# A mixture-of-experts kernel's first transfers and warm-up moved ahead of its engine block, and its last wait moved behind it

## What is computed

```python
def _L0_cond_ref(h, gating_probs, shared_gate_prob, Wg, Wu, Wd, Sg, Su, Sd):   # E, F = 8, 512
    g = jnp.einsum('bsd,edf->ebsf', h, Wg)
    u = jnp.einsum('bsd,edf->ebsf', h, Wu)
    expert_outs = jnp.einsum('ebsf,efd->ebsd', jax.nn.silu(g) * u, Wd)
    expert_output = jnp.einsum('be,ebsd->bsd', gating_probs, expert_outs)
    shared = jnp.einsum('bsf,fd->bsd', jax.nn.silu(h @ Sg) * (h @ Su), Sd)
    sg = shared_gate_prob[:, :, None]
    return (1.0 - sg) * expert_output + sg * shared
x = x + _L0_cond_ref(x, fside_Bx8_0, condB_sharedgateprob[:, None], ...)       # x: (16, 128, 128) f32
x = x + jnp.einsum('bij,bjk->bik', T[itok_B_1_98 - 1], x)
```

## Time and profile before

| | |
|---|---|
| median of 3 runs | 307.45 us (307.35 to 308.07) |
| the profiled execution's own time | 307.27 us |
| its span, first to last instruction of the program | 305.4 us |
| time of that execution outside the span (307.27 - 305.4) | 1.87 us |
| PE busy | 302.0 us, 99% of the span |
| DVE, ACT, POOL busy | 70%, 54%, 34% |

### The profile page before, as it was taken

How to read it: one execution, slowest core, us unless ns; L and a number is a source line. 1 busy time by engine, 2 the same in 40 slices (tenths; PEclk the granted TensorE clock), 3 DMA queues, 4 the chain that set the end, 5 groups by cost and what they waited for, 6 DMA issues and landing times.

```text
span 305.4 us, 4487 instructions
## 1 busy us (share of the span) xinstructions
PE 302.0 (99%) x1348; PEld 250.4 (82%) x1348; DVE 214.1 (70%) x347; ACT 163.8 (54%) x306; POOL 104.8 (34%) x119
## 2 busy tenths in 40 slices
PE   8999999999999999999999999999999999999996
PEld 7888888888888888888888888888888888888885
DVE  4777667766776676667766776677676667787873
ACT  5755555555555555555555555555555555554563
POOL 3687114431244115511551134411451155710010
PEclk9999999999999999999999999999999999999999
DMA  6700200030002000110003000003000000013243
GB/s 192 264 2 1 103 3 0 0 104 0 0 0 103 0 0 0 31 72 0 0 0 112 26 26 26 26 25 106 0 0 2 0 0 0 2 34 69 38 103 103
DMA packets 14186, 12.00 MB, mean 39 GB/s; under 512 B 7008, under 2 KB 12384, under 8 KB 14176
## 3 DMA queue, kind: packets, MB, share of 16 engines
q1 hardware_dynamic: 14032, 11.81, 12.6%
q10 hardware_dynamic: 144, 0.07, 0.1%
HBM read 10.04 MB, written 1.84 MB: 39 GB/s over the span
## 4 chain that ended last, share of the span: by engine, by line
PE 99%; ACT 0%; issue 0%
PE o_bank L499 11%; PE o_bank L496 11%; PE o_bank L497 11%; PE u_bank L468 11%; PE u_bank L470 11%; PE u_bank L469 11%; PE g_bank L468 11%; PE g_bank L470 11%; PE g_bank L469 11%; PE o_bank L535 1%; PE o_bank L514 0%; PE g_bank L514 0%; PE u_bank L514 0%; PE g_bank L542 0%; PE u_bank L509 0%; PE u_bank L542 0%
## 5 line engine op out<-in xcount | busy, mean ns | idle before, releaser
L374 DVE TENSOR_TENSOR u_bank<-u_bank,silu_g 128x512 f32<-128x512 f32 x144 | 100.7, 699 | 82.0 <-PE u_bank L470 81.1
L303 ACT ACTIVATE silu_g<-g_bank 128x512 f32<-128x512 f32 x144 | 86.3, 599 | 132.8 <-PE g_bank L470 132.7
L266 POOL TENSOR_TENSOR acc<-acc,scaled 128x512 f32<-128x512 f32 x32 | 41.4, 1295 | 180.5 <-DVE scaled L388 180.5
L380 DVE TENSOR_TENSOR h_lo<-u_bank,h_hi 128x512 fp32r<-128x512 f32 x144 | 98.1, 681 | 0.1
L309 ACT ACTIVATE h_hi<-u_bank 128x512 fp32r<-128x512 f32 x144 | 85.6, 594 | 0.4 <-DVE u_bank L374 0.4
L499 PE MATMUL o_bank<-h_lo,w_hi 128*128 128x512 f32 x144 | 56.1, 390 | 0.0
L496 PE MATMUL o_bank<-h_hi,w_hi 128*128 128x512 f32 x144 | 56.1, 390 | 0.0
L497 PE MATMUL o_bank<-h_hi,w_lo 128*128 128x512 f32 x144 | 56.0, 389 | 0.0
L469 PE MATMUL u_bank<-x_lo,w_hi 128*128 128x512 f32 x143 | 55.6, 389 | 0.0
L468 PE MATMUL u_bank<-x_hi,w_hi 128*128 128x512 f32 x143 | 55.6, 389 | 0.0
L470 PE MATMUL u_bank<-x_hi,w_lo 128*128 128x512 f32 x143 | 55.6, 389 | 0.0
(11 more groups left out here) (64 smaller groups left out, 145.8 us busy)
## 6 DMA issues: line engine op xcount, KB each, us to landing
w_raw<-in_W_all SPq DMA_DIRECT2D x8, 768.0 KB, 4.4
T_plus<-in_TT SPq DMA_DIRECT2D x16, 64.0 KB, 1.7
turned_y<-yB SPq DMA_DIRECT2D x3, 256.0 KB, 2.3
y<-turned_y SPq DMA_DIRECT2D x12, 64.0 KB, 2.3
acc<-in_xT SPq DMA_DIRECT2D x2, 256.0 KB, 3.6
acc<-in_xT SPq DMA_DIRECT2D x1, 512.0 KB, 5.9
out_y<-res SPq DMA_DIRECT2D x2, 256.0 KB, 2.3
out_y<-res SPq DMA_DIRECT2D x3, 128.0 KB, 1.9
```

The lines of the kernel that those rows point to most:

```text
L266: nc.gpsimd.tensor_tensor(acc[:, t, :], acc[:, t, :], scaled[:, t % 2, :], ALU.add).then_inc(acc_done, 1)
L303: nc.scalar.activation(silu_g[:, k % 2, :], g_bank[k % 2][:, :], ACT.Silu).then_inc(g_read, 1)
L374: nc.vector.tensor_tensor(u_bank[k % HR][:, :], u_bank[k % HR][:, :], silu_g[:, k % 2, :], ALU.mult).then_inc(h_done, 1)
L380: nc.vector.tensor_tensor(h_lo[:, k % HR, :], u_bank[k % HR][:, :], h_hi[:, k % HR, :].bitcast(F32), ALU.subtract).then_inc(split_done, 1)
```

## The change

Three things are moved. The transfers of x tile 0 and of chunk 0's gate and up weights, which SP issued first in its part of the block, are issued in front of the block. The eight warm-up matmuls are too. The wait for the seven stores goes from the end of SP's part to behind the block.

```diff
-        block = ctx.enter_context(nc.Block())
+        nc.sync.dma_start(acc[:, 0, :], xT[0, :, :]).then_inc(x_in[0], 16)
+        nc.sync.dma_start(w_raw[:, 0, 0, 0:2, :], W_gu0[:, :, :]).then_inc(wc0_in[0], 16)
+
+        nought = nc.const_aps.tensor(0.0, (P, P), F32)
+        for _ in range(8):
+            nc.tensor.matmul(o_bank[1][:, 0:P], nought, nought, start=True, stop=True)
+
+        with nc.Block() as block:
...
-            load_x(0, 1, x_in[0])
-            sp.dma_start(w_raw[:, 0, 0, 0:2, :], W_gu0[:, :, :]).then_inc(wc0_in[0], 16)
...
-            sp.wait_ge(stored, 16 * 7)
...
-            def warm_up(n):
-
-                for _ in range(n):
-                    nc.tensor.matmul(o_bank[1][:, 0:P], nought, nought, start=True, stop=True)
-
-            nought = nc.const_aps.tensor(0.0, (P, P), F32)
-            warm_up(8)
...
+        nc.sync.wait_ge(stored, 16 * 7)
```

More of the change, by code:

```diff
@@ L207, in _ @@
[L207 to L294, removed]
-            add_group(E * NT - 1, NT - 1)
@@ L297, in _ @@
-        @block.scalar
-        def _(act):
-            def silu(n, k):
-                act.wait_ge(g_done, n + 1)
-                nc.scalar.activation(silu_g[:, k % 2, :], g_bank[k % 2][:, :], ACT.Silu).then_inc(g_read, 1)
-            def round_h(n, k):
-                act.wait_ge(h_done, n + 1)
-                nc.scalar.activation(h_hi[:, k % HR, :], u_bank[k % HR][:, :], ACT.Copy).then_inc(h_rounded, 1)
-            def copy_y(i):
-                b, nb = parts[i]
-                act.wait_ge(y_turned, i - SINGLE + 1)
-                nc.scalar.activation(y[:, b:b + nb, :], part_bank(i)[:, 0:nb * D].rearrange("p (b d) -> p b d", b=nb),
-                                     ACT.Copy).then_inc(y_done, 1)
-            def round_x(t):
-                act.wait_ge(x_in[min(t, 2)], 16)
-                nc.scalar.activation(x_hi[:, t, :], acc[:, t, :], ACT.Copy).then_inc(x_rounded, 1)
-            def round_w0(c, m):
-                nc.scalar.activation(w_hi[:, 0, c, m, :], w_raw[:, 0, c, m, :], ACT.Copy).then_inc(w0_rounded, 1)
-            act.wait_ge(zero_done, 1)
-            nc.scalar.activation(silu_0[:, :], zero[:, 0:1], ACT.Silu)
-            act.wait_ge(wc0_in[0], 16)
-            for m in range(2):
-                round_w0(0, m)
-            act.wait_ge(wc0_in[1], 16)
-            round_w0(1, slice(0, 2))
-            silu(0, 0)
-            act.wait_ge(wd0_in, 16)
-            round_w0(slice(0, 2), 2)
-            silu(1, 1)
-            round_h(0, 0)
-            round_w0(slice(2, NC), 2)
-            round_x(1)
-            for n in range(2, PEEL_ACT):
-                silu(n, n)
-                round_h(n - 1, n - 1)
-                if n >= PEEL_ACT - 2:
-                    round_x(NT - PEEL_ACT + n)
-            with act.Fori(0, N - U, U) as n0:
-                for k in range(PEEL_ACT, U + PEEL_ACT):
-                    silu(n0 + k, k)
-                    round_h(n0 + k - 1, k - 1)
-            for n in range(N - U + PEEL_ACT, N + 1):
-                if n < N:
-                    silu(n, n)
-                round_h(n - 1, n - 1)
-            def copy_late(i):
-                b, nb = parts[i]
-                act.wait_ge(r_done, i + 1)
-                nc.scalar.activation(res[:, b:b + nb, :], part_bank(i)[:, 0:nb * D].rearrange("p (b d) -> p b d", b=nb),
-                                     ACT.Copy).then_inc(late_done, 1)
-            copy_late(1)
-            copy_late(HALF)
-            for i in range(SINGLE, len(parts)):
-                copy_y(i)
-            copy_late(SINGLE + 1)
-            copy_late(SINGLE + 3)
-            act.wait_ge(late_done, 4)
-            act.dma_start(out[:, B - 1:B, :], res[:, B - 1:B, :]).then_inc(stored, 16)
@@ L464, in _ @@
-        @block.tensor
-        def _(pe):
-            def product(bank, w, x_h, x_l, start, stop):
-                nc.tensor.matmul(bank, w_hi[:, w[0], w[1], w[2], :], x_h, start=start, stop=False)
-                nc.tensor.matmul(bank, w_hi[:, w[0], w[1], w[2], :], x_l, start=False, stop=False)
-                return nc.tensor.matmul(bank, w_lo[:, w[0], w[1], w[2], :], x_h, start=False, stop=stop)
-            def project_g(n, k, at):
-                slot, t, c = at
-                pe.wait_ge(g_read, n - 1)
-                product(g_bank[k % 2][:, :], (slot, c, 0), x_hi[:, t, :], x_lo[:, t, :],
-                        True, True).then_inc(g_done, 1)
-            def project_u(n, k, at, scaled_x=False):
-                slot, t, c = at
-                xt = NT if scaled_x else t
-                if k >= LAG:
-                    pe.wait_ge(split_done, EARLY + n + 1 - HR)
-                product(u_bank[k % HR][:, :], (slot, c, 1), x_hi[:, xt, :], x_lo[:, xt, :],
-                        True, True).then_inc(u_done, 1)
-            def project_down(n, k, at):
-                w = (at[0], at[2], 2)
-                c, slot = k % NC, k % HR
-                bank = o_bank[k // NC % 2]
-                pe.wait_ge(h_rounded, n + 1)
-                nc.tensor.matmul(bank[:, :], w_hi[:, w[0], w[1], w[2], :], h_hi[:, slot, :], start=c == 0, stop=False)
-                nc.tensor.matmul(bank[:, :], w_lo[:, w[0], w[1], w[2], :], h_hi[:, slot, :], start=False, stop=False)
-                pe.wait_ge(split_done, EARLY + n + 1)
-                last = nc.tensor.matmul(bank[:, :], w_hi[:, w[0], w[1], w[2], :], h_lo[:, slot, :],
-                                        start=False, stop=c == NC - 1)
-                if c == NC - 1:
-                    last.then_inc(o_done, 1)
-            def turn_y(i):
-                b, nb = parts[i]
-                pe.wait_ge(yT_done, MOVED * BT + (b - MOVED * BT) // 2 + 1)
-                for j in range(nb):
-                    t, s = (b + j) // BT, ((b + j) % BT) * S
-                    last = nc.tensor.transpose(part_bank(i)[:, j * D:(j + 1) * D], yT[:, t, s:s + S], ident[:, :])
-                last.then_inc(y_turned, 1)
-            def step_b(i, j):
-                b, nb = parts[i]
-                last = nc.tensor.matmul(part_bank(i)[:, j * D:(j + 1) * D], T_plus[:, b + j, :], y[:, b + j, :],
-                                        start=True, stop=True)
-                if j == nb - 1:
-                    last.then_inc(r_done, 1)
-            def wait_step(i):
-                pe.wait_ge(T_done, parts[i][0] // BT + 1)
-                t = parts[i][0] // BT
-                if t < MOVED:
-                    pe.wait_ge(y_in[t], 64)
-                else:
-                    pe.wait_ge(y_done, i - SINGLE + 1)
-            def step_y(i):
-                wait_step(i)
-                for j in range(parts[i][1]):
-                    step_b(i, j)
-            def warm_up(n):
-                for _ in range(n):
-                    nc.tensor.matmul(o_bank[1][:, 0:P], nought, nought, start=True, stop=True)
-            nought = nc.const_aps.tensor(0.0, (P, P), F32)
-            warm_up(8)
-            def opening(x_part, w_part, start, stop):
-                for bank, m in ((g_bank[0], 0), (u_bank[0], 1)):
-                    last = nc.tensor.matmul(bank[:, :], w_part[:, 0, 0, m, :], x_part[:, 0, :], start=start, stop=stop)
-                    if stop:
-                        last.then_inc(u_done if m else g_done, 1)
-            pe.wait_ge(x_rounded, 1)
-            for bank, m in ((g_bank[0], 0), (u_bank[0], 1)):
-                pe.wait_ge(w0_rounded, m + 1)
-                nc.tensor.matmul(bank[:, :], w_hi[:, 0, 0, m, :], x_hi[:, 0, :], start=True, stop=False)
-            pe.wait_ge(split_done, 1)
-            opening(x_lo, w_hi, False, False)
-            pe.wait_ge(w_ready, 1)
-            opening(x_hi, w_lo, False, True)
-            pe.wait_ge(w0_rounded, 3)
-            nc.tensor.matmul(g_bank[1][:, :], w_hi[:, 0, 1, 0, :], x_hi[:, 0, :], start=True, stop=False)
-            nc.tensor.matmul(g_bank[1][:, :], w_hi[:, 0, 1, 0, :], x_lo[:, 0, :], start=False, stop=False)
-            pe.wait_ge(split_done, 2)
-            nc.tensor.matmul(g_bank[1][:, :], w_lo[:, 0, 1, 0, :], x_hi[:, 0, :], start=False, stop=True).then_inc(g_done, 1)
-            project_u(1, 1, place(1))
-            with pe.Fori(0, E - 2, 2) as e:
-                for k in range(LAG, 2 * U + LAG):
-                    if k == LAG:
-                        pe.wait_ge(split_done, EARLY)
-                    if k == LAG + 1:
-                        pe.wait_ge(w_ready, 2)
-                    if k % U == 0:
-                        pe.wait_ge(w_ready, NC * (e + k // U + 1))
-                    if k in range(NC, U, NC):
-                        pe.wait_ge(acc_done, k // NC)
-                    project_g(e * U + k, k, place(k))
-                    project_u(e * U + k, k, place(k))
-                    if k == LAG:
-                        pe.wait_ge(w_ready, 3)
-                    if k == LAG + 2:
-                        pe.wait_ge(w_ready, NC)
-                    project_down(e * U + k - LAG, k - LAG, place(k - LAG))
```

(33 more changed lines are left out.)

460 lines of the change are left out of this document (378 added, 82 removed).

## The result

| | before | changed |
|---|---|---|
| median | 307.94 us (307.35 to 308.22, 6 executions) | 306.83 us (306.46 to 307.02, 6 executions) |
| profiled execution: time, span, outside the span | 307.27, 305.4, 1.87 us | 306.99, 305.7, 1.29 us |

The medians are 1.1 us apart. The ratio of the executions is 0.9973 with a 95% interval of 0.996 to 0.9985, that is 0.8 us less (0.5 to 1.2). That is within the 0.3% that the prediction set as its bound, but the interval excludes "no change". The prediction had three executions of before (307.35, 307.45, 308.07); with three more the median is 307.94. The forecast of 307.1 us rested on 307.45, so its level was helped by that low base; the difference, 0.35 us forecast, was 0.8.

A forecast was written before the change was run, and what follows sets the result against it. The prediction took PE to bound the kernel, busy 302.0 of 305.4 us, with only the short opening and end open. Its terms, -0.35 + 0 + 0 = -0.35 us, took 307.45 to 307.1 us; range 306.6 to 307.6.

The forecast's parts named there:

- The wait, -0.35 us in the span: Program end: closing barrier runs under the last store's landing, removing branch, gap and barrier behind it; -0.35 us (0.25 to 0.45).
- The two transfers, 0: Program start: first transfers still wait for the opening barrier, so moving them ahead of the block gives 0.
- Rival 3: SP's start: an instruction fetch behind the moved branch halts SP between two issues, 0.8 us slower, 307.9 us; chance 0.05.
- rival 4: SP's start: first transfers leave before the barrier ends, 0.5 us more gain, 306.6 us; chance 0.03.
- The warm-up, 0: PE's start: the warm-up matmuls still follow the barrier and start near 0.78 us; 0, bounds -0.05 to +0.05 us.
- The part outside the span, 0: Outside the program: the 1.87 us in front and behind stay, since SP must do its own share and is last.
- Rival 1: Behind the program: engines released early close under the stores, 0.25 us more gain, 306.85 us, at most 306.2; chance 0.13.
- Rival 2: Program end gives nothing: hidden closing work needs about 0.35 us, or stores land later; 307.45 us; chance 0.09.
- The level, 307.1 us: Whole kernel: forecast median, 307.45 us of before less 0.35 us; chance 0.70.
- Within 0.3%: Whole kernel: the median differs from before by no more than 0.3%, about 0.92 us; chance 0.93.

The follow-up runs named there:

- E3: Changed kernel with the wait for the stores back inside the block, only transfers and warm-up ahead of it: 307.77 us, ratio 1.0 to before.
- E2: Changed kernel with transfers and warm-up back inside the block, only the wait for the stores behind it: 306.61 us, ratio 0.9959 to before.
- E12: The changed kernel run a third time, no edit: 306.73 us beside 307.65 of before, ratio 0.9971.
- E1: The changed kernel run again, no edit: 306.65 us beside 307.84 of before, ratio 0.9964.
- E4: Changed kernel with all five engines, not SP alone, waiting for the stores behind the block: 307.37 us, ratio 0.9983 to before.
- E8: Changed kernel with POOL as well as SP waiting for the stores behind the block: 307.34 us, ratio 0.9979 to before.
- E9: Changed kernel with chunk 0's transfer issued on ACT's queue instead of SP's: 307.07 us, ratio 0.9987 to before.
- E5: Changed kernel with PE as well as SP waiting for the stores behind the block: 307.08 us, ratio 0.9981 to before.
- E7: Changed kernel with ACT as well as SP waiting for the stores behind the block: 306.81 us, ratio 0.9966 to before.

## Why the prediction was right, and where it was not

- *The wait, -0.35 us in the span.* Right. SP's last wait is followed by 17 ns, where by the earlier trace rows 0.35 us followed; the barrier lies at 304.4 with 1.2 us to the landing (1.1 forecast; it is 304.4 and not 303.9 because this execution's whole end came later, by 0.6 us). The medians of the spans agree roughly: 305.95 us for the 74 executions of before, 305.3 to 305.5 for the three sets of the changed kernel. That is 0.45 to 0.65 us, 0.1 to 0.3 more than the rows account for. The traces place this remainder. From the issue of ACT's store to the end of the span it takes 2.3 us in before and 2.4 in E3, which have the wait inside the block, and 1.9 to 2.1 us in all twelve profiles that have it behind. So the end gives 0.35 us, as forecast, and what the spans have beyond that is scatter of the opening (see the last section), by which spans of one kernel differ by over a microsecond.
- *The two transfers, 0.* Right: 0.74, 1.18 and 1.65 us as before, and E3 is equal to before. The branch in its new place left no record here either. Rival 3 (a fetch, 307.9 us) and rival 4 (an issue ahead of the barrier, 306.6 us) are out by the same rows. The rule of the Trainium skill named there (Runtime: NRT & Kernel Launch, section "Instruction fetch mechanics") was not put to the test, since no taken branch shows.
- *The warm-up, 0.* Right, by its start at 0.78 us and by E3. But "with the same start, PE gets its speed at the same time" did not hold from one execution to the next: with that same start the weight loads became fast anywhere between 3.9 and 6.5 us.
- *The part outside the span, 0.* This is the step that failed. "SP must do its own share in any case, and it is last by 1.1 us" took it that as much must follow when SP alone comes last as when all come last together. Less follows: 1.32 us outside with SP last, 1.88 us with POOL last and 1.85 with all five. The sum was -0.35 and should have been -0.35 - 0.52 = -0.87 us. Rival 1 had the mechanism, with a chance of 0.13, and priced it at the program's own barrier, 0.25 us; it measured 0.5. That its 306.85 us meets the measured 306.83 is luck: it too stood on the low base. Rival 2, that the end gives nothing, is out by E2.
- *The level, 307.1 us for 306.83.* It lies in the range, but two errors stood against each other: the base of 307.45 was 0.2 to 0.5 us lower than the later medians of before, and the gain was 0.5 us larger than the forecast one. (The bounds of the three parts add up to 306.9 to 307.45, not to 306.95 to 307.4; nothing hangs on it.) "Within 0.3%", given 0.93, came true with 0.27%, but far closer to the bound than that chance says: E12 has 0.29%, and E1, with 0.36%, is beyond it.

What the Trainium skill (Runtime: NRT & Kernel Launch, section "The ~15µs preamble/postamble breakdown") has, a closing barrier that waits for all engines, fits E4 to E8, in which one late engine is enough to lengthen the time; its figures, 5 us in all by the estimate of the prediction, do not agree with 1.84 us.

## What to carry to other kernels

The last wait of a program needs only one engine: let it stand behind the closing barrier of the block, and put it on the engine behind which the least time follows, here SP and not POOL (0.55 us apart). Read an execution's time less its span as a row of its own; it was steady to 0.1 us where spans scattered by more than a microsecond, and it showed in one profile what medians of many executions showed only faintly. And before pricing an instruction that is moved ahead of a block, look whether anything there really stood in its way: here the barrier was ahead of both places, and nothing was gained.

## What was not expected of the hardware

- The time behind the program depends on which engine leaves it last: with SP, DVE, ACT, PE or POOL waiting to the last, 1.32, 1.44, 1.45, 1.61 and 1.90 us lay outside the span (each of the last four together with SP). Whether engines have closing work of different length or are passed in an order stays open.
- PE's change from slow to fast weight loads (0.33 to 0.19 us) came anywhere between 3.9 and 6.5 us in 13 profiles in which the zeros had started at the same 0.78 us. x tile 0 was used within 0.4 us of one time (3.25 to 3.62, E9 aside).
- An early change of pace did not make a short span. In E5 it came first of all, at 3.9 us, and yet its span of 306.0 us is the longest with the warm-up; in E7 it came at about 4.7, and the span is 305.1, the shortest. In E5 the down weights were late: ACT idled 1.10 us for them, POOL's splitting came after ACT, and PE waited for POOL.

```profile
7.54 0.42 ACT L325 ACTIVATE w_hi<-w_raw 128x256 fp32r<-128x256 f32 x1 [1.10 <-DMA w_raw<-in_W_d]
8.04 0.74 POOL L219 TENSOR_TENSOR w_lo<-w_raw,w_hi 128x256 fp32r<-128x256 f32 x1 [0.39 <-ACT w_hi L325]
...
9.05 0.19 PEld L499 LDWEIGHTS o_bank<-h_hi,w_hi 128*128 128x128 f32 x1 [0.59 <-POOL w_lo L219]
```

In E7 the first of these stands at 6.67 after 0.18 us, and PE did not wait:

```profile
6.67 0.42 ACT L325 ACTIVATE w_hi<-w_raw 128x256 fp32r<-128x256 f32 x1 [0.18 <-DMA w_raw<-in_W_d]
```

So the scatter of the spans has at least two sources, PE's pace and the landing of the weights, and both lie in the first 30 us. From one and the same weight load near 30 us (at 30.19 in before, 31.03 in E5) to the issue of ACT's store all fourteen profiles took 272.9 us, alike to about 0.01 us.
- SP's drain took 128 ns right behind a DMA issue (changed kernel) and 13 ns long after one, ACT's 152 ns in both; neither waited for the store, which landed over a microsecond after them.
- With the first two transfers on two queues at once, x tile 0 and chunk 0 took 0.3 and 0.7 us longer from issue to use than on one queue behind each other (E9 and E12, one profile each).
